# All sixteen score products of an attention tile issued together on four row strips, with new instruction orders

## What is computed

```python
# layer 0: attention of 8 heads of 64 over 512 + 77 keys, gated, then a quantised feed-forward with a convolution
sim = jnp.einsum('bhid,bhjd->bhij', q, k); attn = softmax(sim); out = attn @ v @ Wout
h = bit_linear(x, w1); h = depthwise_conv1d(h, conv_w, conv_b); h = silu(h); y = bit_linear(h, w2)
# layer 1 ("second attention"): 16 heads of 8 over the 77 context tokens, then a mixture of 8 experts, top 2
q = apply_rope(x @ Wq.T + bq); k = apply_rope(ctx @ Wk.T + bk); v = ctx @ Wv.T + bv
scores = jnp.einsum('bhqd,bhkd->bhqk', q, k) * 8 ** -0.5
out = softmax(scores) @ v; y = out @ Wo.T + bo
y = moe(y)                          # router, experts, shared expert
```

## Time and profile before

| | |
|---|---|
| median of 3 runs | 267.66 us (267.06 to 267.77) |
| time of the profiled execution | 267.53 us |
| its span, first to last instruction | 265.7 us |
| PE, DVE, ACT, POOL busy | 96%, 82%, 73%, 12% of the span |
| mean granted PE clock | 0.986 |
| instructions | 5563 |

### The profile page before, as it was taken

The page is one execution under the profiler, slowest core; times in us unless marked ns, Lnnn a source line. Parts: engine busy times, 40 slices in busy tenths (PEclk is TensorE's granted clock), DMA queues, the critical chain, the costliest instruction groups (busy, mean ns, idle before and its releaser), DMA issues.

```text
span 265.7 us, 5563 instructions
## 1 busy us (share of the span) xinstructions
...
## 2 busy tenths in 40 slices
...
GB/s 190 32 242 104 90 331 42 90 4 0 93 1 1 2 17 98 69 0 6 88 4 0 0 2 0 4 0 1 2 0 4 1 4 0 2 0 10 23 10 39
DMA packets 8848, 10.70 MB, mean 40 GB/s; under 512 B 1115, under 2 KB 5877, under 8 KB 8821
## 3 DMA queue, kind: packets, MB, share of 16 engines
...
...
HBM read 4.99 MB, written 0.52 MB: 21 GB/s over the span
## 4 chain that ended last, share of the span: by engine, by line
PE 68%; DVE 17%; issue 7%; ACT 6%; POOL 1%; DVEq 0%; ACTq 0%; POOLq 0%
PE slot L516 19%; PE slot L605 12%; PE slot L586 6%; PE slot L587 6%; PE slot L561 3%; PE slot L754 2%; DVE mx L1145 2%; PE slot L567 2%; ACT S L903 2%; PE slot L748 2%; PE slot L612 2%; DVE RB L1150 2%; PE slot L699 2%; PE slot L742 2%; PE slot L576 2%
## 5 line engine op out<-in xcount | busy, mean ns | idle before, releaser
L1039 DVE TENSOR_REDUCE nm<-slot 128x1 f32<-128x589 f32 x64 | 47.6, 765 | 9.7 <-PE slot L587 9.3
L831 ACT ACTIVATE PR<-slot,nm 128x589 f32<-128x589 f32 x64 | 47.8, 750 | 9.3 <-DVE nm L1039 8.7
L516 PE MATMUL slot<-K,PR 128*128 128x128 f32 (+1 forms) x320 | 44.3, 276 | 0.2
L586 PE MATMUL slot<-KH,Q 128*128 128x296 f32 (+1 forms) x128 | 42.1, 345 | 0.2
L516 PEld LDWEIGHTS slot<-K,PR 128*128 128x128 f32 (+1 forms) x320 | 36.0, 142 | 8.2 <-ACT PR L831 5.0
L605 PE MATMUL slot<-PT,V 128*64 128x256 f32 (+1 forms) x320 | 38.1, 384 | 0.7 <-ACT PT L766 0.7
L766 ACT ACTIVATE PT<-slot 128x640 f32<-128x640 f32 x47 | 32.2, 706 | 8.3 <-PE slot L516 7.3
L587 PE MATMUL slot<-KL,Q 128*128 128x296 f32 (+1 forms) x128 | 36.1, 299 | 0.0
L903 ACT ACTIVATE S<-slot,mx 128x77 f32<-128x77 f32 x128 | 29.4, 371 | 6.2 <-DVE mx L1145 5.6
L605 PEld LDWEIGHTS slot<-PT,V 128*64 128x64 f32 (+1 forms) x320 | 22.1, 137 | 12.3 <-issue 3.5
L586 PEld LDWEIGHTS slot<-KH,Q 128*128 128x128 f32 x128 | 24.2, 189 | 3.6 <-issue 1.4
...
...
## 6 DMA issues: line engine op xcount, KB each, us to landing
...
```

The source lines that it names most:

```text
L516: return pe.transpose(dst, src, ident[0:p, 0:p])
L586: pe.matmul(W[:, K0 + lo:K0 + hi], q, KH[:, g % 4, lo:hi], start=True, stop=False)
L831: act.activation(PR[:, s, :], W[:, K0:K0 + KEYS0], ACT.Exp, bias=nm0[:, s:s + 1], accum_out=sum0[:, b, p * 2 + f, t, e:e + 1]).then_inc(pr ...
L1039: dve.tensor_reduce(nm0[:, s:s + 1], W[:, K0:K0 + KEYS0], AX.X, ALU.max, negate=True).then_inc(max_ready, 1)
```

## The change

Stage F of half 0 of an a4 tile issues nothing any more (it still waits for its two banks). Stage F of half 1 issues the four products of the tile, one on each of the four row strips, into the four banks of both halves. A new semaphore scores1_ready counts a half when its two products are done; DVE's maxima wait for it, and a4 no longer counts in front_done. PLAN is a new one from the first line on, with the same items; of its 33 lines those of the last third are shown, ahead of which the new one differs in order and in who copies what.

```diff
-w:F4 n:P2 a2:F2+5@0 w:A1 a1:F3 n:D3 w:D1 a1:A1 a2:D1 o:F1 o:F0 a4:F2 o:D1 o:D1 a4:F0 n:P2 a2:F7 a1:P1 a4:D1 n:D3 a4:A1 f1:F6 f1:A1 a4:F4
-a4:D1 f1:D1 f2:F6 a4:B a2:D1 f2:F7 a1:P1 a4:A1 f2:A1 a4:D1 a4:B a4:Ca f2:A1 a4:Ca f2:F3 f2:D1 f2:A1 f2:F6+4@2 f2:A2 f2:D1 f2:D2 f2:A1 a4:A1 a4:F0
-f2:D1 a4:B+20@2 f2:A2 f2:A2 a4:D1 a4:F2 f2:D1 f2:D2 a4:D1 a4:A1 f2:D2 f2:A2 a4:B+11@7 a4:Ca a4:A1 f2:D2 f3:F6 f3:F7 f3:D1 a4:Ca f3:D1 f3:A1 f3:F4 a4:B
-a4:F0 f3:Cd f3:F6 a4:D1 a4:Ca f4:F5 f3:A1 a6:F7 f4:A1 f3:D1 f3:D1 a4:A1 f3:Cd f4:B f3:A1 f3:A1 f4:F4 a4:F2 f4:A1 f3:Cd f4:D2 f3:Ca f4:F5 f4:B
...
-a6:D1 a4:F2+8@6 a4:D1 a4:B a4:Cd a4:A1 a6:B a4:B a6:D2 m1:F6 a4:A1 a4:Ca a4:F0 a4:B a4:D1 a4:F4 a4:Cd a4:D1 a6:P2 a6:D3 m1:A1 a4:F6 a4:A1 m3:F2
-a6:F3 m3:D1 a4:A1 a4:D1 m3:A1 a4:A1 a4:B a4:B a4:B a4:Ca m2:F0 a4:Ca m3:D2 m2:A1 a4:Ca a6:D1 a4:F4 m1:F2 m1:A1 a6:B m2:B a4:D1 m3:F2 m2:F6
...
+o:D1 w:F7 w:A1 n:P2 a2:F1+3@0 n:D3 w:D1 o:F4 a2:D1 o:D1 o:F7 a1:A1 o:D1 a4:F2 a4:F4 n:P2 a4:D1 n:D3 a4:A1 f1:F0 a4:D1 f1:A1 a4:B+25@1 f1:D1
+a2:F7 f2:F1 a2:D1 f2:A1 a1:P1 a4:Ca f2:D1 f2:F0 f2:F7+3@6 f2:A1 f2:A1 f2:D1 f2:F6 f2:A2 f2:D1 a4:A1 a4:F0 a4:F2 f2:D2 f2:A1 a4:D1 f2:A2 f2:D2 f2:A2
+a4:A1 f2:D1 a4:B a4:Ca f2:A2 a4:D1 f2:D2 a4:B+25@7 a4:A1 f2:D2 a4:Ca f3:F5 f3:F7+9@4 f3:D1 f3:D1 f3:F4 f3:A1 a4:B a4:Ca a4:F2 f3:Cd f3:A1 a4:F0 a4:D1
+f3:D1 f4:F5 f4:A1 a4:A1 a4:D1 f3:F6 a1:P1 f3:A1 f3:D1 f3:Cd a6:F7 a4:B a4:A1 f4:F4 f4:B f3:Cd a4:Cd f4:F3 f4:A1 f4:B f4:D2 f4:A1 f4:D2 f4:P2
...
+a6:P2 a6:D3 a4:D1 a2:F7 a4:A1 m1:F5 a6:B a2:D1 a4:B+5@6 m1:A1 a6:D2 a4:F4 a4:F6 a4:A1 a6:P2 a4:Cd a4:D1 a4:B a4:Ca a4:A1 a4:D1 a1:P1 a6:D3 a4:A1
+m3:F0 m3:D1 m3:A1 m3:D2 a6:F3 a4:B a4:Ca m1:F1 a4:B m1:A1 a4:Ca a4:F6 a4:F4 m2:F0 a4:D1 a4:D1 a4:A1 a6:D1 a4:B+2@2 m3:F2 a4:Cd a6:B
...
-NTH = {x: n for n, x in enumerate(x for x, stage in ORDER["PE"] if stage == "F")}
+NTH = {x: n for n, x in enumerate(x for x, stage in ORDER["PE"] if stage == "F" and x[0] != "a4")}
...
+                    if h == 0:
+                        return
                     pe.wait_ge(q1_ready, (b * QT + t) // TP + 1)
                     pe.wait_ge(kbd_ready, b + 1)
-                    for n in range(2):
-                        rows = slice((2 * h + n) * 32, (2 * h + n + 1) * 32)
-                        mm = pe.matmul(W[:, n * 512:n * 512 + G1 * C], Q1[rows, t * P:(t + 1) * P], KBD[rows, b],
+                    for g in range(G1):
+                        rows, scores = slice(g * 32, (g + 1) * 32), slot(("a4", b, t, g // 2))
+                        mm = pe.matmul(scores[:, g % 2 * 512:g % 2 * 512 + G1 * C], Q1[rows, t * P:(t + 1) * P], KBD[rows, b],
                                        start=True, stop=True)
+                        if g % 2:
+                            mm.then_inc(scores1_ready, 1)
+                    return
...
-                dve.wait_ge(front_done, NTH[item] + 1)
+                if kind == "a4":
+                    dve.wait_ge(scores1_ready, n)
+                else:
+                    dve.wait_ge(front_done, NTH[item] + 1)
```

More of the change, by code:

```diff
@@ L101 @@
 PLAN = """
[L102 to L120, removed]
@@ L134 @@
[L134 to L137, removed]
+x0:F6 x0:A1 k:F0 q:F7 k:A1 k:F2 k:D1 v:F4 q:A1 v:F0 k:A1 q:D1 k:D1 u:F6 v:Ca u:F2 u:D1 v:Ca u:A1 u:F4 u:F0 u:B u:D1 u:D1
@@ new lines @@
+u:A1 u:D1 u:B u:A1 u:Cd s:D2 u:B u:A1 u:Cd u:F6 u:B u:D1 u:Ca u:F4 u:Ca s:F3 u:A1 u:D1 s:D1 u:A1 v:F2 q:F0 u:B v:Ca
+u:B w:D0 u:F2 u:Ca u:Ca w:P1 k:F6 u:D1 q:A1 u:A1 q:D1 u:F4 u:D1 w:F1 k:A1 u:A1 w:A1 u:B u:Ca k:D1 w:D0 u:B w:P1 u:Ca
+u:F6 w:D1 u:F2 u:D1 u:F0 u:D1 u:F4 u:A1 u:A1 u:D1 u:A1 u:B u:Cd u:B u:Ca u:B u:F6 u:D1 u:Cd x0:D2 u:A1 q:F2 u:D1 q:A1
+u:F0 u:B u:D1 u:A1 w:F3 u:Cd u:B u:F4 u:A1 x0:P2 w:A1 q:D1 w:D1 u:Ca u:D1 u:B u:A1 u:F6 a3:F2 u:Cd u:D1 u:A1 u:B u:Ca
+u:F0 u:B w:D0 k:F4 u:Ca a3:D1 w:P1 u:D1 u:A1 k:A1 u:F2 u:D1 g:F7 w:F6 k:D1 u:B g:D1 u:A1 w:A1 w:D1 u:F4 u:Ca u:B u:D1
@@ new lines @@
+u:Ca u:F0 w:D0 u:A1 w:P1 q:F6 u:F2 u:B x0:D3 q:A1 u:Ca u:D1 u:D1 w:F7 u:A1 w:A1 u:F4 u:A1 q:D1 u:B w:D1 u:D1 u:F6 u:Ca
+u:A1 u:B u:F0 u:D1 u:A1 u:Cd u:B x0:F2 u:Ca u:B u:Cd a3:F4 w:D0 x0:A1 k:F2 u:D1 u:F6 u:A1 w:P1 u:B a3:D1 k:A1 u:D1 u:A1
+w:F5 u:B k:D1 u:Cd w:A1 w:D1 u:F0 u:Ca w:D0 u:F4 q:F2 u:F6 u:D1 u:A1 w:P1 u:D1 u:A1 u:D1 u:B u:A1 u:Cd w:F3 q:A1 u:B
+u:B u:Ca u:F0 w:D0 u:F4 u:D1 u:Ca u:D1 w:P1 q:D1 w:F7 w:A1 u:A1 u:B w:A1 w:D1 u:F2 w:D1 u:A1 o:F6 u:B u:Ca u:D1 o:D1
+u:A1 u:F0 u:Ca u:B u:Ca u:F6 u:D1 u:D1 u:A1 u:F4 o:F3 u:D1 u:B w:D0 u:A1 u:B w:P1 u:Cd o:D1 q:F2 u:A1 u:Ca u:F0 q:A1
@@ new lines @@
+u:F6 u:B u:D1 u:Ca u:A1 q:D1 u:D1 w:F3 w:A1 u:B u:A1 w:D1 u:F4 o:F2 u:Ca n:P2 u:D1 o:D1 u:A1 u:B v:F0 u:Cd n:D3 u:B
+k:F2 v:Ca u:Ca u:F6 k:A1 u:D1 v:F0 u:F4 w:D0 u:A1 v:Ca k:D1 u:B u:D1 w:P1 u:Cd u:A1 u:F2 u:D1 u:A1 k:F0 u:B o:F6 u:Cd
+u:B o:D1 k:A1 n:P2 k:D1 u:Ca v:F7 v:Ca u:F4 u:D1 u:F2 u:A1 u:F6 u:D1 u:D1 u:A1 u:A1 w:D0 w:F0 u:B u:B u:Ca n:D3 w:A1
+u:B u:Cd u:F4 u:D1 f1:F1 w:D1 u:Ca q:F3 f1:A1 u:A1 u:F6 f1:D1 q:A1 u:D1 q:D1 u:B u:F0 f2:F2 u:Ca u:D1 u:F4 u:A1 f2:A1 w:P1
+u:A1 w:F3 u:D1 u:B u:B u:A1 f2:D1 f2:A2 w:A1 f2:D2 u:Ca w:D1 u:B f2:F6 u:Ca u:Cd w:D0 u:F2 u:D1 f2:A1 u:A1 f2:F7 k:F4 a3:P1
@@ new lines @@
+u:F0 f2:D1 u:D1 f2:A1 u:B f2:D1 w:D0 w:P1 w:F6 k:A1 u:A1 u:Ca k:D1 f2:A2 f2:D2 u:B w:A1 w:D1 f2:F7 u:Ca u:F2 f2:A1 u:D1 u:F4
+f2:D1 w:P1 u:F0 u:A1 f2:A2 w:F6 u:D1 u:B f2:A2 f2:D2 u:A1 f2:D2 f3:F7 u:D1 f3:D1 u:B w:A1 u:Ca u:F2 w:D1 u:A1 u:D1 u:Ca u:B
+f3:A1 u:Ca u:F4 f3:F6 f3:F1 u:D1 q:F0 u:A1 u:B f3:D1 u:A1 f3:A1 u:Ca u:B w:D0 f3:D1 f3:Cd u:Ca f3:A1 u:F6 q:A1 u:D1 w:P1 u:F2
+u:D1 w:F5 u:A1 w:A1 f4:F4 q:D1 f3:Cd u:F0 u:B w:D1 f4:A1 u:D1 f4:B u:A1 f4:F5 f4:D2 a3:P1 u:B f3:F4 u:A1 u:Ca u:B f4:A1 u:Cd
@@ new lines @@
+w:D0 u:F6 f4:B f3:D1 w:P1 u:Ca f3:A1 f4:D2 f3:Cd u:F2 u:D1 w:F0 u:D1 f3:Cd f4:P2 u:A1 w:A1 u:F4 f4:F1 u:A1 u:B f4:A1 f4:D3 u:B
+u:D1 f4:B w:D1 f4:F0 u:A1 u:Cd u:B f4:D2 u:F6 u:Ca f4:A1 w:D0 u:Ca u:F2 f4:B u:D1 u:A1 u:D1 w:P1 w:F4 u:A1 u:B f4:D2 u:F0
+w:A1 w:D1 u:F4 u:Ca u:D1 u:A1 o:F6 f4:P2 u:B u:D1 u:B o:F7 u:A1 o:D1 u:Ca u:Ca w:D0 w:P1 u:B f4:D3 a1:F0 u:Ca a1:F6 a1:A1
+o:D1 w:F7 w:A1 n:P2 a2:F1+3@0 n:D3 w:D1 o:F4 a2:D1 o:D1 o:F7 a1:A1 o:D1 a4:F2 a4:F4 n:P2 a4:D1 n:D3 a4:A1 f1:F0 a4:D1 f1:A1 a4:B+25@1 f1:D1
```

21 lines of the change are left out of this document (12 added, 9 removed).

## The result

The changed kernel takes 277.7 us (276.9 to 279.2) against 267.5 before: 1.040 times as long, interval 1.036 to 1.043. The forecast was 272.2, range 265.6 to 275.2. The direction was right, the loss of 10.2 us is more than twice the 4.7 of the sum.

The account below looks back on a forecast made before the run. The prediction took PE to bound the kernel from 20 to 160 us and DVE after 166. Its terms, -0.2 + 3.1 + 0.8 + 1.0 = +4.7 on 267.53, gave 272.2 us, range 265.6 to 275.2.

Parts of the forecast that it names:

- dummies behind f1, net of f2: 25 dummy transposes delay a2's rotation on DVE by 4.3 us; f2 gives 1.2 back: +3.1, bounds 1.3 and 6.0.
- third copy of a4 on DVE: DVE makes one more copy of a4, 0.82 us; ACT's one less hides nothing: +0.8, bounds 0 and 0.8.
- up to f1: Fewer dummies ahead of a2's first product start DVE's rotation and the chain to f1 earlier: -0.2, bounds 0 and -0.67.
- four banks at once: Half 0's products also wait for half 1's banks, so DVE waits longer: +1.0, bounds +3.1 and -4.1.
- PE is no bound after 166 us: From 166 us DVE is the fullest real worker, 46.87 of 51 us from 190 to 241.
- eight products: A tile's scores on four strips take 0.95 us of PE instead of 1.47, worth nothing in the end time.
- the hole: PE waits 2.62 us for DVE's norm between f1's second and third transposes; behind it the clock falls to 0.50.
- The rival that dummy transposes do not bring the clock back: Dummies, a2 and f2 all run at half clock: +7.6, 275.1 us, chance 0.08.
- I take +1.0: Cost chosen for half 0's products waiting for all four banks, between bounds of +3.1 and -4.1.
- The walk through the orders: Found three new DVE waits: maxima of (0,2) 1.0, m3's second part 1.0, maxima of (1,3) 1.1; at most +3.1.
- the other bound: All of DVE's idle time from 190 to 241 us goes, a gain of 4.1 us.
- The two dummies fewer: 3 dummies instead of 5 ahead of a2's first product, 0.112 us each, start DVE's rotation 0.2 earlier.

Follow-up runs that it names:

- the halves apart: Changed kernel's orders, scores two and two, first half's products moved up to the first free pair of banks in seven of eight tiles: 285.6 us.
- the reciprocal first: Kernel with both mends, with a6(1,0)'s reciprocal and product moved ahead of m3(0,0)'s second part on DVE: 272.0 us.
- both mends: Changed kernel with the 25 dummies moved between f1's second and third turn and the copy of a4(1,3,0) given back to ACT: 270.5 us.

## Why the prediction was wrong

The medians make a ladder: 267.5 before; 272.3 with the new orders but without the 25 dummies and the third copy; 275.2 with that copy; 277.7 with the dummies. Against the sum:

| term | forecast | measured |
|---|---|---|
| dummies behind f1, net of f2 | +3.1 | +2.5 |
| third copy of a4 on DVE | +0.8 | +2.9 |
| up to f1, four banks at once (measured: all else in the new orders) | -0.2 + 1.0 | +4.8 |

By each kernel's ratio to its own runs of the kernel before, the three are 3.4, 1.9 and 5.3. Either way the last two are far above their forecast, and the first is near it.

**What held.** PE is no bound after 166 us: eight products take 0.80 us where the prediction had 0.95, and it is worth nothing (two and two in the same orders: the same time). The dummies stand behind the hole; the clock is 0.50 from 176 to 180; a2's second rotation starts at 183.26 against 176.82, 5.4 later beyond the 1.0 that f1 is late, between 2.8 and 6.0; f2's waits are gone; the waits for scores and for m3 are longer. The rival that dummy transposes do not bring the clock back fell: it rose to 1.00 with nothing but transposes on PE since 176.0. The sentence of the Trainium skill behind that rival (TensorE: Matmul & The Clock Gate, Part 4: transposes do not count as busy in the same way) does not agree with the trace here.

The prediction read DVE's 46.87 us as the emptying of PSUM; they hold norms and reciprocals as well, and what PE waited for with the scores was ACT's copies, 3.8 us in four waits.

**The step that failed: "I take +1.0".** The walk through the orders had found three waits of 1.0, 1.0 and 1.1, and they came: 0.85 at the maxima of (0,2), 1.38 at m3's second part, 0.91 at the maxima of (1,3), 3.1 together as the walk said. I took a third of that, because no old wait had to go and because the other bound was a gain of 4.1 from all of DVE's idle time. That bound had no instruction behind it. Beside the three there were others that the walk had not named: 0.28 to 0.63 at four more places from 196 to 221 us, 1.8 together. The cause given for the first was wrong too: PE waited 0.79 us there for ACT's copy, not for f3's dummies:

```profile
197.86 0.80 PE L668 MATMUL slot<-KBD,Q 32*128 32x308 f32 x8 [0.79 <-ACT PT L786]
198.70 0.80 DVE L1155 TENSOR_REDUCE mx<-slot 128x8 f32<-128x616 f32 x1 [0.85 <-PE slot L668]
```

In the kernel that has neither the dummies behind f1 nor the third copy, 4.8 us above the kernel before, DVE's waits are 2.6 for scores, 2.5 for a2's products and 1.9 for m3's second part, where they were 0.3, 0.7 and 0.3. Of the 2.5, 1.4 stand ahead of a2's second rotation, whose product the new order puts behind f1; the prediction had no term for that place without the dummies. That these waits make up the 4.8 is read from the traces; the two runs that were to take some of them away (the halves apart, the reciprocal first) made other waits.

**The term that was mis-sized: the copy.** It was priced by its own duration. It cost that, the time that two late DVE instructions then lose beside POOL, and, without the dummies in the hole, a second fall of the clock behind 1.64 us of idle PE, which the prediction did not have at all: 2.0 to 2.9 us by the medians. The changed kernel has the same fall, 0.50 from 250 to 252 us behind the same wait of 1.64.

**The small ones.** Up to f1: f1's third transpose ends its wait at 176.00 against 174.96, 0.89 of which is the start, so +0.15 and not -0.2. The two dummies fewer gave the 0.2 (1.26 late ahead of them, 1.04 behind); the stretch in which PE is the bound, put at nothing, lost 0.4.

**What stays open.** The strips as such cost nothing in their orders (two and two) and the kernel with them is 24.8 us slower in the old ones, so strips and orders cannot be priced apart, nor the claim on four banks from the rest of the orders. Whether another order would carry four strips without loss is not shown: the best one tried, with both mends, is at 270.5, against 266.4 for the kernel before with its dummies in the same hole.
